# Pairs of score banks in one exp, the last denominators and two transposes in another order, and an ending on VectorE, in a four-layer cross-attention kernel

## The chip, the cores and the metric

The kernel runs on one core of one Trainium2 chip. The metric is device time in microseconds (us), the median of three runs. Engines are called by the names of the profile: PE is TensorE (PEld its weight loads), DVE is VectorE, ACT is ScalarE, POOL is GpSimd, SP issues the DMAs.

## What is computed

Eight sequences (a batch is one of them) pass through four layers of cross-attention with the same context:

```python
x = _L0(x, ctx)           # 16 heads of 64: softmax(q k / 8) v, Wo, + x, layer norm
x = _L1(ctx, x, mask)     # 16 heads of 16, keys = ctx and latents, out, rmsnorm, gelu MLP
x = _L2(x, ctx, mask)     # layer norm, 16 heads of 16, out, layer norm, gelu MLP
x = _L3(x, mask, ctx)     # 16 heads of 8, and with the mean also the spread of the values:
#   mean = softmax(..) v;  ex2 = softmax(..) v*v
#   std  = sqrt(relu(ex2 - mean*mean));  out = (instance_norm(x)*std + mean)*mask
```

Layers 0 and 3 have 256 columns of queries and 256 keys per head. They are the "first and last attention" whose exps the change touches.

## The kernel before

All five engines run their own instruction list, written out by hand, and wait for each other through semaphores. There is no scheduler: the order in the Python source of each engine is the order on the chip.

**Stages.** The list of one batch `b` is: projections of layer 1, its attention (`attention12`, L = 1), its MLP, the attention of layer 2, its MLP, and then the mixed stretch (`mixed`), in which layer 3 of batch `b` and layer 0 of batch `b + 1` alternate. Projections of the coming batch (`fill`) are put between the steps of the other stages as filling for PE.

**Scores and exps.** A step `k` of layer 0 or 3 makes the scores of a pair into the two PSUM banks `SC[0]` and `SC[1]` (`scores0`, `scores3`; L700 and L706, L794 and L798). ACT takes the exp of each bank, 512 columns, into one of the four slots of `Pr` (L1219 in layer 0, L1221 in layer 3, which has a bias column), and counts `p_ready` up after each. The next step's scores wait for `p_ready` of their own bank. The values are applied a step later (`pv0` L723, `pv3` L815). `pr_taken` keeps an exp from a slot of `Pr` that is still read.

**Row maxima.** Ahead of the scores, PE computes the same scores in bf16 for the maxima into two banks `MX` (L624, L639 and L645, L659 and L665), DVE reduces them (L1436), PE transposes the result (L678, L681, the units called "T"), and DVE copies the transposed maxima to `nmT` (L1423), which the scores of that group wait for.

**Denominators of layer 0.** Eight pairs of probability tiles are to be summed. POOL adds the two halves of a tile pair (`additions0`, L1769) into `Psum` for the first seven, PE sums over partitions from `Psum` (`denominators` L744), and the eighth pair comes straight from `Pr` (L741, twice as many matmuls). The table `BOTH` says in which step of the mixed stretch each of these stands: a row is (layer, step, units after the scores, units at the step's end). `("den", 3)`, the last denominators, stand at the end of step (3, 0). The table is read by PE, DVE and ACT alike.

**Layer 2's attention.** On PE the projection `k3` (L1091) stands between the scores of the first group and the transposed maxima of the second. On DVE, `quotient(b, 2, 0)` (L445, L1526, L1527: a reciprocal and a product) stands ahead of the copy of the maxima of layer 0's second group (L1423), for which `scores0(b + 1, 2)` waits (L700).

**The end of the program.** Layer 3's sums go to DRAM and back (`scratch`, `C3`), DVE takes a reciprocal (L1582), POOL makes the variance in five steps (L1709 to L1713), ACT loads the table of Sqrt and takes the root (L1261), then loads that of Exp again (L1262), and POOL makes the output in three steps (L1718 to L1720), which SP stores (L510). In the middle batches the same work lies beside the next batch's.

Of the kernel before, what the change touches and what calls it, by code (L numbers as in the profile page):

```python
# [29 lines left out]
B = 8  # L30
# [33 lines left out]
def alone(L):  # L64
# [8 lines left out]
        (3, 0, [], [("den", 3), (3, 1, 2)]),  # L73
        (3, 1, [(3, 1, "T"), ("recip", 1, 0)], [(0, 0, "B")]),
# [105 lines left out]
def build(nc, z_in, ctxT_in, ctx_in, mask1, mask2, mask3, w0, wo, w1qk, w1v, w1o, w1a, w1b,  # L180
          w2qkv, w2o, w2a, w2b, w3, cols_in, rows_in, ident_in, hmask_in, sel_in, out):
    with ExitStack() as stack:
# [127 lines left out]
        def row(name):  # L310
# [32 lines left out]
        v_step, p_step, f_step, x_step, v_apart, p_apart, n_apart, x_apart = (  # L343
            sem(n) for n in ("v_step", "p_step", "f_step", "x_step", "v_apart", "p_apart", "n_apart", "x_apart"))
# [106 lines left out]
        class Chain:  # L451
# [16 lines left out]
            def end(self):  # L468
                assert self.n == self.per_batch, self.n

# [98 lines left out]
        def _(pe):  # L569
# [159 lines left out]
            def denominators(b, m):  # L729
# [5 lines left out]
                pe.wait_ge(ps_ready, 7 * b + min(2 * m + 2, 7))  # L735
                n = SC_AT[b, 0, 14]
                for j in range(4):
                    dst = bank[32 * j:32 * j + 32, 0:D]
                    if m == 3 and j >= 2:
                        for kc in range(2):  # L740
                            mm = pe.matmul(dst, sums2[:, i, :], Pr[:, (n + j - 2) % 4, kc * D:kc * D + D],  # L741
                                           start=(i == 0), stop=True, skip_group_check=True)
                    else:
                        mm = pe.matmul(dst, sums2[:, i, :],  # L744
                                       Psum[:, (2 * m + j // 2) % 4, j % 2 * D:j % 2 * D + D],
                                       start=(i == 0), stop=True, skip_group_check=True)
# [202 lines left out]
            def body(b):  # L949
# [138 lines left out]
                def before2(i):  # L1088
                    if i == 0:
# [3 lines left out]
                def after2(i):  # L1093
                    if more:
# [3 lines left out]
                            lambda g, u: fill("vp3") if u == 0 and g == 0 else None, before2, after2)  # L1098
# [46 lines left out]
        def _(act):  # L1145
# [62 lines left out]
            def mixed(b, steps):  # L1208
                mix = mix_of(b)
                for i in steps:  # L1210
# [4 lines left out]
                    for j in range(2):  # L1215
# [41 lines left out]
            def std3(b):  # L1257
# [4 lines left out]
                act.activation(warm[:], half[:], ACT.Exp)  # L1262
# [127 lines left out]
            moments3(B - 1)  # L1390
            std3(B - 1)
# [3 lines left out]
        def _(dve):  # L1395
# [188 lines left out]
            def body(b):  # L1584
# [53 lines left out]
                quotient(b, 2, 0)  # L1638
                if more:
                    maxima(b + 1, 0, 1, "T")  # L1640
                quotient(b, 2, 1)
# [53 lines left out]
            end3(B - 1)  # L1695


        @block.gpsimd
        def _(pool):
# [5 lines left out]
            def end3(b):  # L1705

                ending.begin(b)
                pool.wait_ge(s_c3, b + 1)
                ending.step(pool.tensor_tensor(C3[:, 0, :], C3[:, 0, :], C3[:, 2, :], ALU.mult))  # L1709
                ending.step(pool.tensor_tensor(C3[:, 1, :], C3[:, 1, :], C3[:, 2, :], ALU.mult))  # L1710
                ending.step(pool.tensor_tensor(C3[:, 2, :], C3[:, 0, :], C3[:, 0, :], ALU.mult))
                ending.step(pool.tensor_tensor(C3[:, 1, :], C3[:, 1, :], C3[:, 2, :], ALU.subtract))
                pool.tensor_scalar(C3[:, 1, :], C3[:, 1, :], 0.0, None, ALU.max).then_inc(s_v, 1)  # L1713

            def output3(b):
                pool.wait_ge(s_std, b + 1)
                pool.wait_ge(s_xn, b + 1)
                ending.step(pool.tensor_tensor(C3[:, 3, :], C3[:, 3, :], xn[:], ALU.mult))  # L1718
                ending.step(pool.tensor_tensor(C3[:, 3, :], C3[:, 3, :], C3[:, 0, :], ALU.add))
                pool.tensor_tensor(C3[:, 3, :], C3[:, 3, :], m3[:], ALU.mult).then_inc(s_o3, 1)  # L1720
                ending.end()
# [51 lines left out]
            def body(b):  # L1773
# [37 lines left out]
                if not is_last(b):  # L1811
                    additions0(b + 1, [4, 5, 6])
# [108 lines left out]
```

## Time and profile before

| | us |
|---|---|
| median of 3 runs (1083.14 to 1083.92) | 1083.77 |
| the profiled execution | 1082.43 |
| its span, first to last instruction | 1080.6 |
| PE busy in it | 966.1 |
| DVE busy | 541.7 |
| ACT busy | 485.9 |
| POOL busy | 269.8 |
| one middle batch (start to start) | 126.0 |

The span is that of the profiled execution; what lies around it is 1.8 us. Busy times are sums of instruction durations. A matmul's duration runs past the start of the next, so the distance between the starts of two rows is what a group of matmuls costs PE, and that is how such rows are read below. "Idle" in brackets at the end of a row is how long the engine stood before it, and whose instruction released it.

### The profile page before, as it was taken

Reading aid. Unit: us, or ns where it says so; the run is one execution under the profiler, and the core shown is the slowest. Engines: PE = TensorE matmul, PEld = TensorE weight load, DVE = VectorE, ACT = ScalarE, POOL = GpSimd, SP = SyncE. Lnnn points to the kernel's source line nnn. Section 1 sums busy time; section 2 is a strip of 40 time slices with the busy share of each in tenths; the row PEclk is TensorE's granted clock in tenths of the full one; section 3 lists DMA queues with packets and bytes.
Section 4 is the critical chain, followed back from the end, with each engine's and each line's share of the span. In section 5 each row is a group of like instructions: output and inputs, shape, how many; then the busy total and the mean of one; then the engine's idle time right before and its main releaser. Section 6 shows DMA issues by size and latency. Waiting matters only on the chain.

```text
span 1080.6 us, 21561 instructions
## 1 busy us (share of the span) xinstructions
PE 966.1 (89%) x8592; PEld 603.1 (56%) x8592; DVE 541.7 (50%) x1028; ACT 485.9 (45%) x937; POOL 269.8 (25%) x389
## 2 busy tenths in 40 slices
PE   7989999999999999999999999999999999985671
PEld 5566663766455664666636665556646666344420
DVE  3343564455645565455644555455654556443440
ACT  2424453453534545445534545345454455433233
POOL 0220230242211611233202422116212332023203
PEclk9999999999999999999999999999999999988786
DMA  9300230011300212102300103002111022002000
GB/s 371 140 1 1 79 107 19 18 39 47 107 31 6 79 38 76 36 1 84 107 19 18 47 38 107 32 5 83 42 67 35 2 84 98 19 19 78 5 9 32
DMA packets 29058, 60.15 MB, mean 56 GB/s; under 512 B 9376, under 2 KB 21024, under 8 KB 24096
## 3 DMA queue, kind: packets, MB, share of 16 engines
q1 hardware_dynamic: 28960, 58.77, 15.1%
q8 instruction: 70, 1.15, 0.4%
q14 instruction: 28, 0.23, 0.1%
HBM read 53.52 MB, written 5.24 MB: 54 GB/s over the span
## 4 chain that ended last, share of the span: by engine, by line
PE 74%; DVE 10%; issue 10%; ACT 4%; POOL 2%; DMA 1%; POOLq 0%; SPq 0%; DVEq 0%; ACTq 0%
PE GP L584 6%; PE GP L992 6%; PE PV L723 6%; PE GP L1003 5%; PE GP L586 5%; PE SC L706 4%; DVE nm L1436 4%; PE SC L798 4%; PE GP L976 3%; PE PV L769 3%; PE GP L815 3%; PE SC L910 3%; PE GP L591 2%; PE PV L923 2%; PE GP L592 2%
## 5 line engine op out<-in xcount | busy, mean ns | idle before, releaser
L1436 DVE TENSOR_REDUCE nm<-MX 128x2 bf16<-128x512 f32 (+1 forms) x352 | 227.1, 689 | 152.2 <-PE MX L645 65.0
L1221 ACT ACTIVATE Pr<-SC,bcol 128x512 f32<-128x512 f32 x128 | 80.9, 683 | 132.9 <-PE SC L798 132.9
L584 PE MATMUL GP<-zP,W 128*128 128x128 f32 x512 | 106.9, 291 | 7.0 <-DMA W<-w 6.9
L1769 POOL TENSOR_TENSOR Psum<-Pr 128x512 f32<-128x512 f32 x56 | 71.3, 1273 | 163.6 <-ACT Pr L1219 163.6
L1219 ACT ACTIVATE Pr<-SC 128x512 f32<-128x512 f32 x128 | 69.2, 592 | 80.6 <-PE SC L706 80.6
L586 PE MATMUL GP<-uP,W 128*128 128x128 f32 x512 | 100.4, 278 | 0.0
L584 PEld LDWEIGHTS GP<-zP,W 128*128 128x128 f32 x512 | 78.9, 194 | 28.4 <-issue 26.7
L1253 ACT ACTIVATE Pr<-SC,bcol 128x512 f32<-128x512 f32 x96 | 60.7, 684 | 58.1 <-PE SC L910 58.1
L1737 POOL TENSOR_TENSOR stat<-stat,half 128x1 f32<-128x1 f32 x24 | 13.7, 569 | 269.8 <-DVE stat L1616 172.7
L586 PEld LDWEIGHTS GP<-uP,W 128*128 128x128 f32 x512 | 79.2, 195 | 0.0
L1003 PE MATMUL GP<-WB,work 128*128 128x256 f32 x256 | 60.8, 386 | 10.5 <-DVE work L1564 10.5
L723 PE MATMUL PV<-Pr,V 128*64 128x256 f32 x512 | 69.4, 392 | 0.8
L798 PE MATMUL SC<-work,K 64*128 64x512 f32 x256 | 67.7, 598 | 0.0
L1742 POOL TENSOR_TENSOR stat<-stat,half 128x2 f32<-128x2 f32 x8 | 5.7, 709 | 245.4 <-DVE stat L1492 245.4
L706 PE MATMUL SC<-Q,K 64*128 64x256 f32 x512 | 65.7, 376 | 0.0
L992 PE MATMUL GP<-oT,WA 128*128 128x128 f32 x512 | 64.0, 285 | 1.1 <-issue 0.8
L992 PEld LDWEIGHTS GP<-oT,WA 128*128 128x128 f32 x512 | 61.2, 199 | 5.0 <-issue 3.3
L1003 PEld LDWEIGHTS GP<-WB,work 128*128 128x128 f32 x256 | 46.8, 190 | 21.9 <-issue 16.5
L910 PE MATMUL SC<-work,K 64*128 64x512 f32 x192 | 54.3, 636 | 0.0
L1157 ACT ACTIVATE Q<-GP,cols 128x256 f32<-128x256 f32 x56 | 23.5, 470 | 68.4 <-PE GP L586 68.4
L1552 DVE TENSOR_TENSOR work<-GP,cols 128x512 f32<-128x512 f32 x32 | 22.1, 692 | 61.3 <-PE GP L992 61.3
L706 PEld LDWEIGHTS SC<-Q,K 64*128 64x128 f32 x512 | 49.3, 189 | 5.0
(194 smaller groups left out, 1727.4 us busy)
## 6 DMA issues: line engine op xcount, KB each, us to landing
WA<-w1a SPq DMA_DIRECT2D x8, 1024.0 KB, 4.8
WB<-w1b SPq DMA_DIRECT2D x8, 1024.0 KB, 7.0
WA<-w2a SPq DMA_DIRECT2D x8, 1024.0 KB, 5.0
WB<-w2b SPq DMA_DIRECT2D x8, 1024.0 KB, 7.1
W<-w SPq DMA_DIRECT2D x6, 1024.0 KB, 9.9
scratch<-U SPq DMA_DIRECT2D x16, 256.0 KB, 2.0
C<-scratch SPq DMA_DIRECT2D x96, 32.0 KB
zP<-z_in SPq DMA_DIRECT2D x8, 128.0 KB, 4.2
```

The lines of the kernel that those rows point to most:

```text
L584: pe.matmul(dst, W0[:, piece, 2 * s, at:at + P], zP[:, s * P:s * P + P], start=True, stop=False)
L586: mm = pe.matmul(dst, W0[:, piece, 2 * s + 1, at:at + P], uP[:, s * P:s * P + P], start=False, stop=True)
L706: mm = pe.matmul(SC[r][:, kc * D:kc * D + D], K0[half, k, kc * P:kc * P + P], Q0[half, k, :], start=False, stop=True, skip_group_check=True)
L723: mm = pe.matmul(bank[64 * j:64 * j + 64, i * D:i * D + D], V0[:, kc, h * 64:h * 64 + 64], Pr[:, (n + j) % 4, kc * D:kc * D + D], start=(k ...
L798: pe.matmul(SC[j][:].rearrange("p (t l) -> p t l", l=D), K3[half, g % 2, kc * P:kc * P + P], Q3[half, g // 2 * 2:g // 2 * 2 + 2, :], start ...
L910: pe.matmul(SC[r][:].rearrange("p (t l) -> p t l", l=P), K[half, c, kc * P:kc * P + P], Q12[half, 4 * c:4 * c + 4, :], start=False, stop=True,
L992: mm = pe.matmul(g[:, j * P:j * P + P], WA[:, c, f * P:f * P + P], oT[:, c, :], start=(c == 0), stop=(c == 1), skip_group_check=True)
L1003: mm = pe.matmul(g[:, 0:D], G[:, f * P:f * P + P], WB[:, f, :], start=(f == 0), stop=(f == 7))
L1219: act.activation(Pr[:, (n + j) % 4, :], SC[j], ACT.Exp, scale=0.125).then_inc(p_ready, 1)
L1221: act.activation(Pr[:, (n + j) % 4, :], SC[j], ACT.Exp, bias=bcol[:, 3 + k % 2:4 + k % 2], scale=8.0 ** -0.5).then_inc(p_ready, 1)
L1436: dve.tensor_reduce(dst, MX[(n + i) % 2][:].rearrange("p (a k) -> p a k", a=a), AX_X, ALU.max, negate=True).then_inc(mx_done, 1)
L1769: pool.tensor_tensor(Psum[:, c % 4, :].rearrange("p (a l) -> p a l", l=D), two[:, :, 0:D], two[:, :, D:2 * D], ALU.add)\
```

## The change

There are six edits.

1. In layers 0 and 3, ACT takes the exp of both score banks in one instruction of 1024 columns, once both banks are full, and counts `p_ready` up by two after it. There are 128 of these in place of 256 of 512 columns. Layers 1 and 2 keep theirs.
2. POOL adds the eighth pair too (64 additions L1769 in place of 56), and PE's last denominators come from `Psum` (four matmuls in place of six: the two L744 and four L741 become four of the first kind). The waits on `ps_ready` are renumbered, and ACT's wait on `den_done` goes.
3. `("den", 3)` moves from the end of step (3, 0) to the middle of step (3, 1), behind its scores.
4. `k3` moves from behind the scores of layer 2's first group to ahead of the maxima of its second group.
5. On DVE the copy of the maxima of layer 0's second group moves ahead of `quotient(b, 2, 0)`.
6. The last batch's eight steps on `C3` run on DVE in place of POOL. The Sqrt table is loaded by an extra small instruction right after `moments3`, and the last batch's return to the Exp table goes.

```diff
-        (3, 0, [], [("den", 3), (3, 1, 2)]),
-        (3, 1, [(3, 1, "T"), ("recip", 1, 0)], [(0, 0, "B")]),
+        (3, 0, [], [(3, 1, 2)]),
+        (3, 1, [("den", 3), (3, 1, "T"), ("recip", 1, 0)], [(0, 0, "B")]),
...
-                eng.wait_ge(ps_ready, 7 * b + min(u // 2 + 1, 7))
-                if u // 2 == 7:
-                    eng.wait_ge(den_done, 4 * b + 4)
+                eng.wait_ge(ps_ready, 8 * b + u // 2 + 1)
...
+        def variance3(eng, ending, b):
+            ending.begin(b)
+            ending.step(eng.tensor_tensor(C3[:, 0, :], C3[:, 0, :], C3[:, 2, :], ALU.mult))
...
+            eng.tensor_scalar(C3[:, 1, :], C3[:, 1, :], 0.0, None, ALU.max).then_inc(s_v, 1)
+        def scaled3(eng, ending):
+            ending.step(eng.tensor_tensor(C3[:, 3, :], C3[:, 3, :], xn[:], ALU.mult))
...
-                pe.wait_ge(ps_ready, 7 * b + min(2 * m + 2, 7))
-                n = SC_AT[b, 0, 14]
+                pe.wait_ge(ps_ready, 8 * b + 2 * m + 2)
                 for j in range(4):
                     dst = bank[32 * j:32 * j + 32, 0:D]
-                    if m == 3 and j >= 2:
-                        for kc in range(2):
-                            mm = pe.matmul(dst, sums2[:, i, :], Pr[:, (n + j - 2) % 4, kc * D:kc * D + D],
-                                           start=(i == 0), stop=True, skip_group_check=True)
...
-                def before2(i):
-                    if i == 0:
+                def amid2(g, u):
+                    if (g, u) == (0, 0):
+                        fill("vp3")
+                    if (g, u) == (0, "T"):
                         g, full = begin("k3", (ld_w3, 16))
...
+                    if L in (0, 3):
+                        act.wait_ge(sc_full, n + 2)
+                        pr_taken(act, n, 1)
+                        pr_taken(act, n + 1, 1)
+                        act.activation(Pr[:, n % 4:n % 4 + 2, :], SCP[:], ACT.Exp,
+                                       bias=bcol[:, 3 + k % 2:4 + k % 2] if L else 0.0,
+                                       scale=8.0 ** -0.5 if L else 0.125).then_inc(p_ready, 2)
...
-                act.activation(warm[:], half[:], ACT.Exp)
+                if not is_last(b):
+                    act.activation(warm[:], half[:], ACT.Exp)
...
             moments3(B - 1)
+            act.activation(warm[:], ident[:, 0:1], ACT.Sqrt)
             std3(B - 1)
...
+                if more:
+                    maxima(b + 1, 0, 1, "T")
                 quotient(b, 2, 0)
-                if more:
-                    maxima(b + 1, 0, 1, "T")
...
-                    additions0(b + 1, [4, 5, 6])
+                    additions0(b + 1, [4, 5, 6, 7])
...
             end3(B - 1)
+            last = Chain(dve, last_step, F_STEPS)
+            dve.wait_ge(s_c3, B)
+            variance3(dve, last, 0)
+            dve.wait_ge(s_std, B)
+            dve.wait_ge(s_xn, B)
+            scaled3(dve, last)
```

How the lists of the engines stand, before and now. First PE in the mixed stretch, from the values of step (0, 7) to the transposed maxima of step (3, 1); before:

```order
L723 MATMUL PV<-Pr,V 64x256 x3
L744 MATMUL PV<-Psum,sums 32x256 [waits ps_ready]
L744 MATMUL PV<-Psum,sums 32x256
L741 MATMUL PV<-Pr,sums 32x256 x4
L639 MATMUL MX<-b3row,sel 128x512 [waits mx_done]
L639 MATMUL MX<-b3row,sel 128x512
L645 MATMUL MX<-K3b,Q3b 128x256 x4
L794 MATMUL SC<-nmT,sel 128x256 [waits p_ready] x2
L794 MATMUL SC<-nmT,sel 128x256 x2
L798 MATMUL SC<-work,K 128x512 x2
L678 MATMUL MX<-identb,nm 128x128 [waits mx_done]
L678 MATMUL MX<-identb,nm 128x128
```

And in the changed kernel:

```order
L737 MATMUL PV<-Pr,V 64x256 [waits p_ready]
L737 MATMUL PV<-Pr,V 64x256 x3
L653 MATMUL MX<-b3row,sel 128x512 [waits mx_done]
L653 MATMUL MX<-b3row,sel 128x512
L659 MATMUL MX<-K3b,Q3b 128x256 x4
L801 MATMUL SC<-nmT,sel 128x256 [waits p_ready] x2
L801 MATMUL SC<-nmT,sel 128x256 x2
L805 MATMUL SC<-work,K 128x512 x2
L752 MATMUL PV<-Psum,sums 32x256 [waits ps_ready]
L752 MATMUL PV<-Psum,sums 32x256 x3
L692 MATMUL MX<-identb,nm 128x128 [waits mx_done]
L692 MATMUL MX<-identb,nm 128x128
```

The last denominators (32x256) stood ahead of the maxima and the scores of step (3, 1); they now stand behind them and ahead of the transposes, as four matmuls. `Psum` is POOL's sum, `sums` the ones that sum over partitions.

Next DVE behind layer 2's attention (`U<-PV` and `Ax` are the quotient, `nmT<-MX 128x256` is the copy of the maxima of layer 0); before:

```order
L1436 TENSOR_REDUCE nm<-MX 128x2 [waits mx_full0,mx_full1]
L1436 TENSOR_REDUCE nm<-MX 128x2
L445 TENSOR_TENSOR gate<-half 128x1 [waits v_apart,pv_done,s_Ax]
L1526 RECIPROCAL U<-PV 128x128
L1527 TENSOR_TENSOR Ax<-PV,U 128x128 [waits v_step]
L1423 COPY nmT<-MX 128x256 [waits mx_full1]
L445 TENSOR_TENSOR gate<-half 128x1 [waits v_apart,pv_done,s_Ax]
L1526 RECIPROCAL U<-PV 128x128
L1527 TENSOR_TENSOR Ax<-PV,U 128x128 [waits v_step]
```

And in the changed kernel:

```order
L1455 TENSOR_REDUCE nm<-MX 128x2 [waits mx_full0,mx_full1]
L1455 TENSOR_REDUCE nm<-MX 128x2
L1442 COPY nmT<-MX 128x256 [waits mx_full1]
L443 TENSOR_TENSOR gate<-half 128x1 [waits v_apart,pv_done,s_Ax]
L1545 RECIPROCAL U<-PV 128x128
L1546 TENSOR_TENSOR Ax<-PV,U 128x128 [waits v_step]
L443 TENSOR_TENSOR gate<-half 128x1 [waits v_apart,pv_done,s_Ax]
L1545 RECIPROCAL U<-PV 128x128
L1546 TENSOR_TENSOR Ax<-PV,U 128x128 [waits v_step]
```

The copy moved up over one quotient's three instructions.

Last ACT at the end of the program (`C<-C` is the root, `warm` a column that only calls for a table); before:

```order
L1182 ACTIVATE Ax,stat<-m 128x256 [waits s_nst]
L1261 ACT_TABLE_LOAD [waits st_out,s_v]
L1261 ACTIVATE C<-C 128x256 [waits s_nst]
L1262 ACT_TABLE_LOAD
L1262 ACTIVATE warm<-half 128x1
```

And in the changed kernel:

```order
L1192 ACTIVATE Ax,stat<-m 128x256 [waits s_nst]
L1409 ACT_TABLE_LOAD
L1409 ACTIVATE warm<-ident 128x1 [waits s_nst]
L1278 ACTIVATE C<-C 128x256 [waits st_out,s_v]
```

The table load that stood between the wait for `s_v` and the root now stands ahead of that wait.

## Rows read from the trace of the kernel before

**Rows 1.** Windows, two batches: us, busy PE, PEld, DVE, ACT, POOL; clock, DMA

```profile
198.00:324.00 126.00, 119.10 (x1077) 74.30 (x1076) 67.41 (x129) 60.89 (x118) 33.85 (x48) 1.00 0.14 49
...
954.00:1081.00 127.00, 74.29 (x644) 43.85 (x642) 46.71 (x89) 41.36 (x78) 28.56 (x49) 0.81 0.08 27
```

**Rows 2.** Page, the chain that ended last, shares by engine

```profile
PE 74%; DVE 10%; issue 10%; ACT 4%; POOL 2%; DMA 1%; POOLq 0%; SPq 0%; DVEq 0%; ACTq 0%
```

**Rows 3.** Timeline, TensorE, batch 3: start, us, line, what, count [idle <-releaser]

```profile
537.82 0.64 PE L744 MATMUL PV<-Psum,sums 128*32 128x256 f32 x8
538.39 0.29 PE L678 MATMUL MX<-identb,nm 128*128 128x128 bf16 x2
...
540.07 0.38 PE L794 MATMUL SC<-nmT,sel 64*128 64x256 bf16 x4
...
541.24 1.08 PE L723 MATMUL PV<-Pr,V 128*64 128x256 f32 x8
542.25 0.41 PE L744 MATMUL PV<-Psum,sums 128*32 128x256 f32 x2
...
543.26 0.39 PE L639 MATMUL MX<-b3row,sel 64*128 64x512 bf16 x2
...
543.71 0.38 PE L794 MATMUL SC<-nmT,sel 64*128 64x256 bf16 x4
...
545.45 0.27 PE L678 MATMUL MX<-identb,nm 128*128 128x128 bf16 x2 [0.50 <-DVE nm L1436]
```

**Rows 4.** Timeline, same place: GpSimd, ScalarE, VectorE

```profile
536.45 1.27 POOL L1769 TENSOR_TENSOR Psum<-Pr 128x512 f32<-128x512 f32 x1 [1.37 <-ACT Pr L1219]
...
541.35 1.26 ACT L1221 ACTIVATE Pr<-SC,bcol 128x512 f32<-128x512 f32 x2 [1.43 <-PE SC L798]
...
544.01 1.29 DVE L1436 TENSOR_REDUCE nm<-MX 128x2 bf16<-128x512 f32 x2 [2.35 <-PE MX L645]
```

**Rows 5.** Timeline, TensorE, the end of the third attention

```profile
503.56 0.70 PE L1091 MATMUL GP<-uC,W 128*128 128x256 f32 x2
504.09 0.22 PE L681 MATMUL MX<-identb,nm 128*128 128x128 bf16 x1
...
507.22 0.29 PE L678 MATMUL MX<-identb,nm 128*128 128x128 bf16 x2
...
509.02 0.39 PE L700 MATMUL SC<-nmT,sel 64*128 64x512 bf16 x2 [0.50 <-DVE nmT L1423]
...
510.20 1.13 PE L984 MATMUL GP<-W2O,Ax 128*128 128x256 f32 x4
511.44 1.08 PE L723 MATMUL PV<-Pr,V 128*64 128x256 f32 x8
...
515.44 0.71 PE L1110 MATMUL GP<-W,uC 128*128 128x128 f32 x4 [0.32 <-ACT Q L1157]
```

**Rows 6.** Timeline, VectorE, the same stretch

```profile
508.68 0.28 DVE L1423 COPY nmT<-MX 128x256 bf16<-128x256 bf16 x1
...
509.93 0.29 DVE L1527 TENSOR_TENSOR Ax<-PV,U 128x128 f32<-128x128 f32 x1
```

**Rows 7.** Timeline, all engines, the end of the program

```profile
1070.33 0.72 POOL L1709 TENSOR_TENSOR C<-C 128x256 f32<-128x256 f32 x1 [3.47 <-DVE C L1582]
...
1074.37 1.28 ACT L1261 ACT_TABLE_LOAD   x1 [12.21 <-issue]
...
1076.16 0.72 POOL L1718 TENSOR_TENSOR C<-C,xm 128x256 f32<-128x256 f32 x1 [1.86 <-ACT C L1261]
...
1078.51 0.34 SPq L510 DMA_DIRECT2D out<-C  x1
```

**Rows 8.** Groups by line and shape: busy us, mean ns, idle before

```profile
L1219 ACT ACTIVATE Pr<-SC 128x512 f32<-128x512 f32 x128 | 69.2, 592 | 80.6 <-PE SC L706 80.6
...
L1613 DVE TENSOR_TENSOR xa<-GP,res 128x256 f32<-128x256 f32 x8 | 3.4, 425 | 8.8 <-PE GP L984 8.8
...
L1621 DVE TENSOR_SCALAR xb<-xa,stat 128x256 f32<-128x256 f32 x8 | 2.8, 353 | 4.1 <-POOL stat L1737 4.1
```

More of the change, by code:

```diff
@@ L469, in end @@
                 assert self.n == self.per_batch, self.n
+        def variance3(eng, ending, b):
+            ending.begin(b)
+            ending.step(eng.tensor_tensor(C3[:, 0, :], C3[:, 0, :], C3[:, 2, :], ALU.mult))
+            ending.step(eng.tensor_tensor(C3[:, 1, :], C3[:, 1, :], C3[:, 2, :], ALU.mult))
+            ending.step(eng.tensor_tensor(C3[:, 2, :], C3[:, 0, :], C3[:, 0, :], ALU.mult))
+            ending.step(eng.tensor_tensor(C3[:, 1, :], C3[:, 1, :], C3[:, 2, :], ALU.subtract))
+            eng.tensor_scalar(C3[:, 1, :], C3[:, 1, :], 0.0, None, ALU.max).then_inc(s_v, 1)
+        def scaled3(eng, ending):
+            ending.step(eng.tensor_tensor(C3[:, 3, :], C3[:, 3, :], xn[:], ALU.mult))
+            ending.step(eng.tensor_tensor(C3[:, 3, :], C3[:, 3, :], C3[:, 0, :], ALU.add))
+            eng.tensor_tensor(C3[:, 3, :], C3[:, 3, :], m3[:], ALU.mult).then_inc(s_o3, 1)
+            ending.end()
         def shifts(b, L, g):
@@ L734, in denominators @@
                     wait(pe, *pv_bank_taken(b, "den", half))
-                pe.wait_ge(ps_ready, 7 * b + min(2 * m + 2, 7))
-                n = SC_AT[b, 0, 14]
+                pe.wait_ge(ps_ready, 8 * b + 2 * m + 2)
                 for j in range(4):
                     dst = bank[32 * j:32 * j + 32, 0:D]
-                    if m == 3 and j >= 2:
-                        for kc in range(2):
-                            mm = pe.matmul(dst, sums2[:, i, :], Pr[:, (n + j - 2) % 4, kc * D:kc * D + D],
-                                           start=(i == 0), stop=True, skip_group_check=True)
[L743 to L746, printed above, removed]
+                    mm = pe.matmul(dst, sums2[:, i, :], Psum[:, (2 * m + j // 2) % 4, j % 2 * D:j % 2 * D + D],
+                                   start=(i == 0), stop=True, skip_group_check=True)
                 mm.then_inc(den_done, 1)
@@ L1097, in body @@
                 attention12(b, 2, make, K2, lambda g, t, kc: V2[:, slot(g, t):slot(g, t) + 32], (s_V2, b + 1),
-                            lambda g, u: fill("vp3") if u == 0 and g == 0 else None, before2, after2)
+                            amid2, after=after2)
                 if more:
@@ L1214, in mixed @@
                         queries3(b, [(Q3, 0), (Q3, 1)])
-                    for j in range(2):
+                    if L in (0, 3):
[5 more added lines that the diff above has]
+                                       scale=8.0 ** -0.5 if L else 0.125).then_inc(p_ready, 2)
+                    for j in range(0 if L in (0, 3) else 2):
                         act.wait_ge(sc_full, n + j + 1)
@@ L1637, in body @@
                     maxima(b + 1, 0, 1, 2)
-                quotient(b, 2, 0)
                 if more:
                     maxima(b + 1, 0, 1, "T")
+                quotient(b, 2, 0)
                 quotient(b, 2, 1)
@@ L1705, in end3 @@
             def end3(b):
-                ending.begin(b)
                 pool.wait_ge(s_c3, b + 1)
[L1709 to L1713, printed above, removed]
+                variance3(pool, ending, b)
             def output3(b):
@@ L1717, in output3 @@
                 pool.wait_ge(s_xn, b + 1)
[L1718 to L1721, printed above, removed]
+                scaled3(pool, ending)
             def blocks12(b, L):
@@ L1825, in _ @@
             pool.wait_ge(const_p, 3)
-            additions0(0, range(7))
+            additions0(0, range(8))
             power0(0)
```

6 lines of the change are left out of this document (2 added, 4 removed).

## The prediction

> **What bounds the kernel now.** I read four views, in this order: windows by batch, the chain that ended last, the timeline around each moved instruction, and the timeline of the program's end. In a middle batch PE is busy 119.1 of 126.0 us at full clock, and no other engine passes 67.4; in the last batch PE is busy 74.3 of 127 us and the granted clock averages 0.81 [rows 1]. The chain that ended last is PE for 74% [rows 2]. So seven of eight batches are PE's list plus the few places in which PE stands, and the last batch and the end of the program are latencies, one engine after another. ACT is busy 60.9 of 126 us: shortening it pays only where PE waits for an exp. What counts is what leaves PE's list, which of PE's gaps is filled, and what leaves the chain at the end.
>
> **Edits 2 and 3: the last denominators.** They cost PE from 542.25 to 543.26, 1.01 us; the denominators that come from `Psum` alone cost from 537.82 to 538.39, 0.57 [rows 3]. So the form saves 0.44. The move saves more. Today the transposes at 545.45 wait 0.50 for DVE's reductions, which start 0.75 behind the maxima (543.26 to 544.01) and let PE go 1.44 after their start [rows 3, 4]. In the new order, from 542.25: maxima 0.45 (543.26 to 543.71), scores 1.17 (as 540.07 to 541.24), denominators 0.57, together 2.19 [rows 3]; DVE's side is 0.75 + 1.44 = 2.19 as well. The transposes start at 544.44 in place of 545.45: 1.0 us less, because the denominators now lie in the gap. Behind them the list is the same and relative to itself, so the gain stays. Seven mixed stretches have these denominators: 7.0 us. Bounds: 0 (something else catches up at once) and 1.0 each; I take 1.0, since both sides of the row agree. The first batch's prologue has no such gap and saves the form alone, 0.4.
>
> What the edit can spoil: POOL's eighth addition must be done before them. An addition takes 1.27 and starts about as the exp ends [rows 4]; the scores of step (0, 7) are in by 537.82, where the next work starts [rows 3], their exp by 539.0, so `Psum` is ready near 540.3, 3.5 us ahead of its new reader. In the prologue the reader is not moved, and there one addition can be late, 1.27 at most and once. ACT no longer waits for `den_done`, which the move would otherwise have made late.
>
> **Edit 5: the copy ahead of the quotient.** The transposed maxima are made at 507.22, but DVE copies them at 508.68 behind a quotient, and the scores stand 0.50 for it until 509.02 [rows 5, 6]. With the copy first (near 507.5) the scores start at 508.5 when PE is free. The second quotient, which ends at 510.22 today (509.93 + 0.29, rows 6), ends 0.1 later, since it gains the copy's place and loses the copy's wait; the second half of the output projection can go at about 510.5, as today within 0.2 us. The next thing PE waited for is the exp of these scores: the values at 511.44 come 1.24 behind the projection at 510.20 [rows 5], and they follow the exp, so they come 0.45 earlier. The `v3` matmuls at 515.44 waited 0.32 for ACT's `Q` [rows 5], which follows the filling behind these values, so they follow too. Gain 0.45, bounds 0.15 (layer norm after the second quotient holds the rest) and 0.5; seven times, 3.2 us.
>
> **Edit 4: `k3`.** It costs PE 503.56 to 504.09, 0.53 [rows 5]. It leaves a place between scores and transposes that wait for DVE's two reductions (1.3 us, as in rows 4), and goes to one where PE stands for DVE's copy of the transposed maxima. It fills one gap and opens another, both set by DVE: I take 0.04 each, 0.3 in all, nearest to nothing; bounds 0 and 0.53 each, its whole cost hidden.
>
> **Edit 1: one exp over two banks.** One exp of 512 columns is 592 ns [rows 8], the pair with a bias 1.26 us [rows 4]. The trace has no exp of 1024 columns: it costs at least one (0.68) and at most two separately (1.37 with the bias); I take 1.12, the pair without one start, nearest to the 1.26. The Trainium skill, "ScalarE: Activation LUTs", section "What ACT_TABLE_LOAD costs", gives 280 ns and 0.833 ns a column with a pointer bias, an estimate of 1.13 us; by it the sum below is the same. The one exp starts when the second bank is full, about 0.1 later, and ends about when the second does today. The first bank comes free 0.4 later, and that is the price where PE has nothing else. Tightest is step (3, 1): exp from 541.45 to 542.57 against scores at 542.70. The slack is 0.1. In the other steps maxima and values (over 1 us) lie between. In the last four steps of the last batch the chain runs through both exps and scores, and shortens by some 0.05 each. Denominators (0, 5) behind a slightly later evacuation may lose 0.05 a batch. Net I take a loss of 0.2, bounds +2 and -2.
>
> **Edit 6: the end.** From 1070.33 to 1074.37 are POOL's five steps, 4.04 us; then the table 1.28; the root to 1076.16; then three steps, 2.35, to 1078.51 [rows 7]. Nearest DVE rows at 256 columns: 425 ns for two tensors, 353 ns with a scalar [rows 8]; with 0.04 for a wait on itself, five steps are 4 x 0.46 + 0.35 = 2.2, three are 1.35. The table load goes under ACT's idle stretch of 12.21 [rows 7]. Gain 1.85 + 1.28 + 1.0 = 4.1, bounds 3.3 (DVE's steps at 0.6 each) and 4.5. The load row, 1.28, stands with ACT idle before and the root right behind. The Trainium skill, same page and section, puts about 1.38 us of drain to each switch, which would make 5.5; the distance from 1074.37 to 1076.16 has no room for it.
>
> **The sum.** 7.0 + 0.4 + 3.2 + 0.3 - 0.2 + 4.1 = 14.8. The profiled execution took 1082.43 us, so 1067.6; it was 1.3 below the median, so **1069 us**.
>
> The last batch starts 11 us earlier, and there PE works at half clock (1.2 of 2.4 GHz) in parts: a mean of 0.81 over 127 us is up to 48 us at half, so 24 lost at most, of which 14 by PE's busy share of 74.3 in 127 [rows 1]. Which matmuls fall there may change; a fifth of it is 3 us either way. The Trainium skill, "TensorE: Matmul & The Clock Gate", part 1, says that PE's activity releases the throttle; the trace agrees (1.00 where PE is busy 119 of 126, rows 1), and it changes no term here.
>
> **Rivals.**
> - *The gains on PE are taken back by the next wait.* For it: DVE and ACT sit close behind PE in the mixed stretch, both sides of my 2.19 are equal, and one tenth of slack stands at (3, 1). Against: behind each place PE runs on without idle in the rows. Then remain the form, 0.44 x 8 = 3.5, the quotient at its lower bound 1.1, the end 4.1: 8.7, so 1075.
> - *Only the end pays.* If every gap re-forms (POOL's longer list holds the denominators, edit 5 delays layer norm), 4.1: 1079.6.
> - *The exp over both banks holds PE, slower.* PE starts the next scores on the first bank while ACT is on the second; now they wait for both. If PE has nothing between, each step costs 0.44 (the later release of bank 0). It decides from 14.8 / 0.44 = 34 of the 128 steps. If half of them, 64, are such steps: 28 us, 1097. For it: the closed ring at the end of the last batch. Against: PE's place after the scores has maxima or values in every middle step.
> - *The switch costs its drain too* and the end gives 5.5: 1067.5.
>
> **How the numbers follow.** Forecast 0.63, gains taken back 0.22, only the end 0.05, exp slower 0.05, drain 0.05. The range reaches from 1065 (drain or a kind clock) to 1076.5 (gains taken back, with an unkind clock). A difference under 0.2%, 2.2 us, could not be told from none by this measurement. Faster by more: 0.93; slower by more: 0.05 (the exp ring); between: 0.02.
>
> **What would show it.** In the new profile: transposes of step (3, 1) about 2.2 us behind the values of step (0, 7) and no idle before them; the period of a middle batch 124.5 in place of 126.0; no wait of layer 0's third scores for the copy; exps of 1024 columns at 1.03 and 1.12; 8.2 us from the reciprocal's end to the store becoming 4.1. I am wrong if the period stays above 125.3, if PE shows new idle before scores released by ACT, or if the exp takes 1.3 and more.

## The result and the profile after

The changed kernel takes 1071.75 us (median of 4 runs, 1070.70 to 1075.57) against 1083.85 (4 runs, 1083.14 to 1085.31): a ratio of 0.9887, 95% interval 0.9867 to 0.9907. The forecast was 1069, range 1065 to 1076.5. So it is faster, by 12.1 us where 14.8 were forecast. The profiled execution took 1071.56 (span 1069.8). Of the runs below, one of the twelve of the copy-first kernel took 1442.0 us at a mean granted clock of 0.62, and it is left out of that kernel's figures.

The windows of a middle and of the last batch, which answer to [rows 1] (the middle one is now 124.4 us wide), and the chain's shares, as [rows 2]:

```profile
196.40:320.80 124.40, 118.49 (x1071) 73.67 (x1071) 67.22 (x128) 59.23 (x102) 35.51 (x50) 1.00 0.14 50
943.20:1069.80 126.60, 77.90 (x647) 45.39 (x645) 49.93 (x97) 38.94 (x69) 24.13 (x42) 0.80 0.08 28
```

```profile
PE 74%; DVE 11%; issue 7%; ACT 4%; POOL 2%; DMA 1%; SPq 0%; DVEq 0%; ACTq 0%; POOLq 0%
```

Where the 10.87 us between the two profiled executions lie I read from the starts of `q1`, the first matmuls of each batch (L976 before, L983 after). Two of them in the profile after, TensorE's timeline:

```profile
442.88 1.38 PE L983 MATMUL GP<-hT,W1QK 128*128 128x128 f32 x9
```

```profile
567.52 1.81 PE L983 MATMUL GP<-hT,W1QK 128*128 128x128 f32 x11
```

| stretch, us | before | after | change | forecast |
|---|---|---|---|---|
| start to the first `q1` | 69.89 | 69.83 | -0.06 | -0.4 |
| a typical middle batch | 125.77 | 124.37 | -1.40 | -1.5 |
| seven batches, first to last `q1` | 879.63 | 869.78 | -9.85 | -10.1 |
| last batch, `q1` to PE's last matmul | 110.46 | 114.07 | +3.61 | -0.2, clock 3 either way |
| PE's last matmul to the end | 20.63 | 16.10 | -4.53 | -4.1 |

(The batch shown is 124.64 long, the longest of the seven; the same one before is 126.05. The 126.0 of the prediction was the width of a window. The forecast's loss of 0.2 for the exp is spread here as its text has it: 0.05 lost in each of eight batches at the denominators (0, 5), 0.05 gained in each of the last four steps.) The middle batches and the end did what was forecast. The miss is nearly all in one row: the last batch, up to PE's last matmul, took 3.6 us longer in these two executions.

**The denominators**, TensorE and ScalarE, the place of [rows 3, 4]:

```profile
536.56 1.08 PE L737 MATMUL PV<-Pr,V 128*64 128x256 f32 x8
537.57 0.39 PE L653 MATMUL MX<-b3row,sel 64*128 64x512 bf16 x2
...
539.19 0.64 PE L752 MATMUL PV<-Psum,sums 128*32 128x256 f32 x8
539.76 0.28 PE L692 MATMUL MX<-identb,nm 128*128 128x128 bf16 x2
```

```profile
536.75 1.11 ACT L1229 ACTIVATE Pr<-SC,bcol 128x1024 f32<-128x1024 f32 x1 [1.52 <-PE SC L805]
```

The values of step (0, 7) start at 536.56, the transposes of (3, 1) at 539.76, 3.20 later; before it was 4.21 (541.24 to 545.45, rows 3). From the end of the values (537.57) it is 2.19, the 2.2 of the forecast. The denominators cost 539.19 to 539.76, 0.57, and the transposes have no idle time in brackets any more. This is the 1.0 of the forecast.

**The copy ahead of the quotient**, VectorE and TensorE, the place of [rows 5, 6]:

```profile
503.23 0.29 DVE L1442 COPY nmT<-MX 128x256 bf16<-128x256 bf16 x1 [1.05 <-PE MX L692]
...
504.49 0.29 DVE L1546 TENSOR_TENSOR Ax<-PV,U 128x128 f32<-128x128 f32 x1
```

```profile
504.14 0.39 PE L714 MATMUL SC<-nmT,sel 64*128 64x512 bf16 x2
```

The copy starts at 503.23, now ahead of the quotient's last step (504.49), and the third scores start at 504.14 without waiting.

**The exps**, groups by form, as [rows 8] (busy us, mean ns):

```profile
L1229 ACT ACTIVATE Pr<-SC,bcol 128x1024 f32<-128x1024 f32 x64 | 71.2, 1113 | 137.0 <-PE SC L805 126.1 <-issue 10.9
L1229 ACT ACTIVATE Pr<-SC 128x1024 f32<-128x1024 f32 x64 | 65.3, 1020 | 81.9 <-PE SC L720 42.4 <-issue 39.5
```

1020 and 1113 ns, where the prediction says 1.03 and 1.12. The Trainium skill, "ScalarE: Activation LUTs", section "What ACT_TABLE_LOAD costs", gives an estimate of 1.04 without the pointer bias and 1.13 with it, both 0.02 too long here.

**The end**, ScalarE, VectorE and SyncE, the place of [rows 7]:

```profile
1055.85 1.28 ACT L1409 ACT_TABLE_LOAD   x1
1057.15 0.20 ACT L1409 ACTIVATE warm<-ident 128x1 f32<-128x1 f32 x1
...
1063.67 0.42 DVE L472 TENSOR_TENSOR C<-C 128x256 f32<-128x256 f32 x1
...
1065.51 0.29 DVE L476 TENSOR_SCALAR C<-C 128x256 f32<-128x256 f32 x1
1065.84 0.42 ACT L1278 ACTIVATE C<-C 128x256 f32<-128x256 f32 x1 [8.49 <-DVE C L476]
...
1067.66 0.34 SPq L524 DMA_DIRECT2D out<-C  x1
```

From the first step behind the reciprocal (1063.67) to the store it is 3.99 us; it was 8.18 before (1070.33 to 1078.51, rows 7). VectorE's five steps take 2.17 to the root's start, as forecast 2.2. The table is loaded at 1055.85, 10 us ahead of the root. The other 0.3 of the 4.53 in the table lies ahead of the reciprocal, which starts 8.19 us behind PE's last matmul in place of 8.51.

### The profile page after: what moved, and what is told of

The parts are those of the page before. It is cut to its first block, busy times and chain, and to the rows that moved or that the text cites. A ratio compares the mean times of both kernels' runs of the same rounds, so it can differ in the third digit from the quotient of the medians.

```text
span 1069.8 us, 21418 instructions
## 1 busy us (share of the span) xinstructions
PE 965.6 (90%) x8560; PEld 600.5 (56%) x8560; DVE 545.0 (51%) x1036; ACT 471.2 (44%) x808; POOL 275.1 (26%) x389
## 4 chain that ended last, share of the span: by engine, by line
PE 74%; DVE 11%; issue 7%; ACT 4%; POOL 2%; DMA 1%; SPq 0%; DVEq 0%; ACTq 0%; POOLq 0%
PE GP L598 6%; PE GP L999 6%; PE PV L737 6%; PE GP L1010 6%; PE GP L600 5%; PE SC L805 5%; DVE nm L1455 4%; PE SC L720 4%; PE GP L983 3%; PE PV L776 3%; PE PV L930 3%; PE GP L822 2%; PE GP L605 2%; PE SC L917 2%; PE MX L653 2%
## 5 line engine op out<-in xcount | busy, mean ns | idle before, releaser
L1229 ACT ACTIVATE Pr<-SC,bcol 128x1024 f32<-128x1024 f32 x64 | 71.2, 1113 | 137.0 <-PE SC L805 126.1
L1786 POOL TENSOR_TENSOR Psum<-Pr 128x512 f32<-128x512 f32 x64 | 81.4, 1272 | 173.6 <-ACT Pr L1229 173.6
L1229 ACT ACTIVATE Pr<-SC 128x1024 f32<-128x1024 f32 x64 | 65.3, 1020 | 81.9 <-PE SC L720 42.4
L1270 ACT ACTIVATE Pr<-SC,bcol 128x512 f32<-128x512 f32 x96 | 60.7, 684 | 58.6 <-PE SC L917 58.6
L1754 POOL TENSOR_TENSOR stat<-stat,half 128x1 f32<-128x1 f32 x24 | 13.7, 569 | 267.7 <-DVE stat L1635 172.5
L1442 DVE COPY nmT<-MX 128x256 bf16<-128x256 bf16 (+1 forms) x96 | 25.8, 269 | 55.1 <-PE MX L692 40.2
L1571 DVE TENSOR_TENSOR work<-GP,cols 128x512 f32<-128x512 f32 x32 | 22.1, 692 | 59.5 <-PE GP L999 59.5
```

The costliest lines, as they stand in the source:

```text
L1229: act.activation(Pr[:, n % 4:n % 4 + 2, :], SCP[:], ACT.Exp, bias=bcol[:, 3 + k % 2:4 + k % 2] if L else 0.0, scale=8.0 ** -0.5 if L else ...
L1270: act.activation(Pr[:, n % 4, :], SC[n % 2][:], ACT.Exp, bias=bias, scale=scale)\
L1786: pool.tensor_tensor(Psum[:, c % 4, :].rearrange("p (a l) -> p a l", l=D), two[:, :, 0:D], two[:, :, D:2 * D], ALU.add)\
```

## The experiments

Each kernel was timed together with the kernel before, and its ratio is to that kernel's times there. "Period" is the length of a typical middle batch. "Half clock" is the time at 1.2 GHz in the last batch's first 100 us or to PE's last matmul, from the granted clock: in a window of 25 us with a mean of 0.86 it is 50 x (1 - 0.86) = 7 us, since the clock granted is either 1.2 or 2.4 GHz.

**One edit at a time, from the kernel before.**

The last denominators, in the new form and at the new place, edits 2 and 3:

```diff
-        (3, 0, [], [("den", 3), (3, 1, 2)]),
-        (3, 1, [(3, 1, "T"), ("recip", 1, 0)], [(0, 0, "B")]),
+        (3, 0, [], [(3, 1, 2)]),
+        (3, 1, [("den", 3), (3, 1, "T"), ("recip", 1, 0)], [(0, 0, "B")]),
...
-            additions0(0, range(7))
+            additions0(0, range(8))
```

> The kernel before with the last denominators alone (edits 2 and 3: from Psum in one pass, and one step later). By the theory that they then lie in the gap before the transposes of step (3, 1): period of a middle batch 125.77 - 1.0 = 124.8, seven times, and 0.2 in the prologue (there the projection of the attention then waits for ScalarE's evacuation): 7.2 us less, about 1076.5. By the rival that the next wait takes the move back: only the form, 0.44 a batch, period 125.3, about 1080.5.

Measured: 1077.67, ratio 0.9932 (0.9919 to 0.9946); period 124.79; seven batches 872.71, 6.92 less. The rival is out.

The form alone, which is edit 2 with the table as before (the expectation calls it edit 3):

```diff
-                    if m == 3 and j >= 2:
...
-            additions0(0, range(7))
+            additions0(0, range(8))
```

> The kernel before with the form alone (edit 3: eight additions and one kind of denominators, at their old place). By my theory PE's list is shorter by 0.44 a batch and the transposes of (3, 1) still wait 0.50 for DVE, whose reductions start with the maxima behind the denominators: period 125.35, 3.3 us in all, about 1080.5. By the rival that POOL's eighth addition (1.27) comes too late for a reader at the old place, about 0.9 behind the values of (0, 7): PE waits up to 0.5 there and the gain is nothing, period 125.8 or more, about 1084.

Measured: 1079.98, ratio 0.9960 (0.9944 to 0.9975); period 125.33, so the form alone is 0.44 and the move 0.54. TensorE's timeline shows both halves:

```profile
541.00 0.64 PE L736 MATMUL PV<-Psum,sums 128*32 128x256 f32 x8
541.57 0.39 PE L637 MATMUL MX<-b3row,sel 64*128 64x512 bf16 x2
...
543.75 0.27 PE L676 MATMUL MX<-identb,nm 128*128 128x128 bf16 x2 [0.50 <-DVE nm L1427]
```

The denominators cost 0.57 at their old place, with no wait for POOL, and the transposes still stand 0.50. The rival, POOL too late, is out.

The copy first, edit 5:

```diff
+                if more:
+                    maxima(b + 1, 0, 1, "T")
                 quotient(b, 2, 0)
-                if more:
-                    maxima(b + 1, 0, 1, "T")
```

> The kernel before with edit 5 alone (the copy of the transposed maxima ahead of the first quotient). By the forecast 0.45 a batch: period 125.3, 3.2 us in all, about 1080.7. By the rival that the second quotient and layer norm take it back: 0.15 a batch, about 1082.8.

Measured: 1083.32 against 1085.12, ratio 0.9983 (0.9969 to 0.9997); period 125.36, 0.41 a batch, 2.93 in the seven. The medians' interval, 0.3 to 3.4 us, has room for both the forecast and the rival; the period, 0.41 against the rival's 0.15, decides for the forecast.

One exp over both banks, edit 1:

```diff
+                    if L in (0, 3):
+                        act.wait_ge(sc_full, n + 2)
...
+                    for j in range(0 if L in (0, 3) else 2):
```

> The kernel before with edit 1 alone (one exp over both banks in the first and the last attention). By the forecast nothing in the middle batches (period 125.8, within 0.1) and within 0.3 in all, about 1084; the last four steps of the last batch stay at 2.50 to 2.55. By the rival that the missing 3 us of the last batch are the exp's, which frees the first bank later: the last batch is 2 to 3 us longer from its first matmul to the end, 1086 to 1087.

Measured: 1085.41 against 1085.12, ratio 1.0006 (0.9993 to 1.0019); period 125.77 and seven batches 879.63, to the hundredth as before. Its cost is in the last steps of the last batch, TensorE's timeline:

```profile
1059.36 0.39 PE L794 MATMUL SC<-nmT,sel 64*128 64x256 bf16 x4 [0.71 <-ACT Pr L1219]
...
1061.90 0.64 PE L815 MATMUL GP<-Pr,V 128*32 128x256 f32 x8 [0.72 <-ACT Pr L1219]
```

The last scores wait 0.71 for the exp, and the last values 2.54 behind them wait for it again; the last six steps are mostly 2.50 apart with two exps of 512 and 2.55 to 2.63 with one (K part to K part). From the first scores of this attention (1038.34) to the first matmul of the last values (1061.90) it is 23.56 against 23.39 with the clock alike: 0.17 lost. In this profile the whole last batch is 112.9 us, 2.5 more than before, which is the rival's number; but the rest of it came with 41.0 us at half clock against 34.1, and the medians of 11 and 23 runs are alike. So the exp costs 0.2 here, and not the missing 3 us.

The end, edit 6:

```diff
             moments3(B - 1)
+            act.activation(warm[:], ident[:, 0:1], ACT.Sqrt)
...
+            variance3(dve, last, 0)
...
-            end3(B - 1)
-            output3(B - 1)
```

> The kernel before with edit 6 alone (the last steps on VectorE, the Sqrt table loaded early). Nothing else moves, so the whole 4.1 us come out at the end: 8.2 from the reciprocal to the store becomes 4.1, about 1079.7. By the rival that the changed end itself costs the last batch its missing 3 us: about 1082.7.

Measured: 1080.83 against 1084.55, ratio 0.9962 (0.9948 to 0.9976), 4.1 us. PE's last matmul to the end: 16.21, 4.4 less. The rival is out.

This run is also a control. Its instructions up to PE's last matmul are those of the kernel before, and still its profiled execution has 113.7 us from the last `q1` to there, 3.3 more than the 110.5 before, with 44.4 us at half clock against 34.1. Two executions of one and the same last batch can differ by nearly as much as the +3.61 of the table.

`k3` moved, edit 4:

```diff
-                def before2(i):
-                    if i == 0:
+                def amid2(g, u):
+                    if (g, u) == (0, 0):
+                        fill("vp3")
+                    if (g, u) == (0, "T"):
                         g, full = begin("k3", (ld_w3, 16))
```

> The kernel before with edit 4 alone (k3 behind the first transposes of the third attention). Middle batches: 0.00 to 0.04 less each. Last batch: k3 stands in front of the second pair of maxima; at half clock that pair starts 0.5 to 0.6 later behind the transposes than in the kernel before, and the second scores some 0.3 later; at full clock under 0.1. In all 0 to 0.5 slower, about 1085.

Measured: 1086.63 against 1083.95, ratio 1.0028 (1.0011 to 1.0046): slower by about 3 us, more than any theory had. In the middle batches nothing (period 125.81, against 125.77; 0.11 us in seven). So all of it is in the last batch. It is not only a lower mean clock: at a mean of 0.973 two executions of this kernel took 1086.49 and 1086.63, and the four of the kernel before timed beside them 1083.60 to 1084.50.

The changed kernel with `k3` back (the reverse of that diff):

> The changed kernel with k3 back at its old place (edit 4 undone). In the middle batches within 0.05 a batch either way (forecast 0.04 gained by the edit), so the period is 124.4 to 124.5. In the last batch k3 is 0.65 us of half-clock work in front of the second pair of maxima: by the theory that the move costs there, the last batch is 0.4 to 0.7 shorter, about 1071.3. By the theory that the clock alone makes the last batch's loss, its length depends on where the half-clock stretches fall, 1070 to 1073 with no direction.

Measured: 1071.21, ratio 0.9875 (0.9859 to 0.9891), period 124.37. The intervals with and without the move overlap, so this run decides for neither theory, and the 3 us of the move alone are not seen between these two medians (1071.75 and 1071.21). The direct cost can be read. TensorE, third attention of the last batch, the changed kernel and then this one:

```profile
990.94 0.27 PE L695 MATMUL MX<-identb,nm 128*128 128x128 bf16 x1 [1.57 <-DVE nm L1455]
991.07 1.19 PE L1101 MATMUL GP<-uC,W 128*128 128x256 f32 x2
992.19 0.61 PE L673 MATMUL MX<-b2row,sel 64*128 64x512 bf16 x2
...
996.28 0.21 PE L913 MATMUL SC<-nmT,sel 64*128 64x128 bf16 x1 [0.70 <-ACT Pr L1270]
996.77 0.39 PE L913 MATMUL SC<-nmT,sel 64*128 64x128 bf16 x7 [0.28 <-ACT Pr L1270]
```

```profile
991.35 0.27 PE L695 MATMUL MX<-identb,nm 128*128 128x128 bf16 x1 [1.57 <-DVE nm L1452]
992.03 0.61 PE L673 MATMUL MX<-b2row,sel 64*128 64x512 bf16 x2 [0.41 <-DVE nmT L1439]
...
995.23 1.22 PE L1098 MATMUL GP<-uC,W 128*128 128x256 f32 x2
...
996.88 0.45 PE L913 MATMUL SC<-nmT,sel 64*128 64x128 bf16 x8 [0.32 <-DVE nmT L1439]
```

Both stretches start at half clock. At its new place `k3` takes 1.12 (991.07 to 992.19) in a gap of 0.41, so the second maxima come 1.25 behind the transposes in place of 0.68. At its old place it lay under the wait for the exp, which now stands open (0.70). The second scores (all but their first matmul) are 5.83 behind the transposes against 5.53: 0.3 lost. The rest of the 3 us of `k3` alone I can't place by a row. More half-clock time followed in the profile of that kernel (58 us against 34), but it is of the slowest of its eight executions (1091.74), which doesn't prove that the move caused it.

**The clock in the last batch.** PE stands there for VectorE and ScalarE in every step. These kernels put matmuls of the identity, whose results nothing reads, into those waits, in the last batch alone. They go to a bank of PSUM that the next real matmuls overwrite:

```diff
+PADS = {"oT": 14, "w2": 8, "yT": 20, "q2": 6, "yT2": 20, "w4": 20, "q3": 4}
...
                     pe.wait_ge(*o.bank_taken(name))
+                    for _ in range(PADS.get(name, 0) if is_last(b) else 0):
+                        pe.matmul(GP[bank][:, 0:P], ident[:], ident[:], start=True, stop=True)
                     for s, v in ready:
```

> The kernel before with 92 matmuls more in the last batch, 128x128 of the identity, put where PE waits for VectorE or ScalarE (14 ahead of oT, 8 of w2, 20 each of yT, yT2 and w4, 6 of q2, 4 of q3), into a bank that the next matmuls overwrite. They compute nothing. If the clock is what the waiting costs, the 41.4 us at half clock in the last batch shrink to under 15 and the last batch gets 3 to 10 us shorter. If the clock doesn't follow PE's activity there, the pads only lengthen the waits: 0 to 4 us longer.

> The changed kernel with the same 92 matmuls in its last batch. By the theory that the missing 3 us of its last batch are half-clock time, both padded kernels have about the same clock there, and the difference between them is the forecast's sum of 13 to 15 us. By the rival that the edits themselves (k3, the exp) cost the last batch 3 us, the difference stays at 12 (1071.75 against 1083.85).

Measured: 1084.55 against 1084.55 (ratio 0.9996, 0.9984 to 1.0008) and 1071.69 (0.9877, 0.9861 to 0.9893), a difference of 12.9. Half clock fell (23.9 and 20.5 us, from 34.1 and 41.0; the 41.4 of the expectation isn't what the profile of the kernel before shows up to PE's last matmul) and the time did not, so neither expectation was met: I had sized a pad at 0.11 us. TensorE's timeline of the changed kernel without pads, then with 92, then with 47:

```profile
983.64 0.41 PE L975 MATMUL GP<-ident,xb 128*128 128x128 f32 x2 [3.04 <-DVE xb L1593]
```

```profile
980.72 4.63 PE L970 MATMUL GP<-ident 128*128 128x128 f32 x40
985.18 0.38 PE L978 MATMUL GP<-ident,xb 128*128 128x128 f32 x2
```

```profile
979.22 2.62 PE L970 MATMUL GP<-ident 128*128 128x128 f32 x22
982.34 0.44 PE L978 MATMUL GP<-ident,xb 128*128 128x128 f32 x2 [0.50 <-DVE xb L1596]
```

Twenty pads take 4.46 (980.72 to 985.18), 0.22 each (the trace has two records for each); the wait was 3.04. So they made the batch wait for them. Eleven end 0.50 before VectorE does. The difference of 12.9 can't be held against 14 or 12: its interval is wider than both.

The run with 47, the changed kernel and `PADS = {"oT": 8, "w2": 4, "yT": 11, "q2": 3, "yT2": 11, "w4": 10}`:

> The changed kernel with 47 matmuls of the identity in the last batch instead of 92 (8 ahead of oT, 4 of w2, 11 of yT, 3 of q2, 11 of yT2, 10 of w4), each 0.23 us, so that at full clock they end within the waits they lie in (2.37, 1.38, 3.04, 0.99, 3.04, 2.87). The theory that the waiting costs clock: half-clock time in the last batch falls to 20 to 25 us as with 92, but now without the 1.0 to 1.5 that the long rows of pads cost, so 2 to 4 us less than the changed kernel, about 1069. The rival, that the clock gained is worth nothing since the batch waits for VectorE and ScalarE: 1071 to 1072.

Measured: 1065.73 (1064.26 to 1067.30), ratio 0.9834 (0.9820 to 0.9848), 6 us less than the changed kernel, with 17.1 us at half clock against 41.0. The rival is out, and the gain is more than the 2 to 4 of the theory.

The next fills the waits for the maxima too, with 31 more, and takes `k3` back:

```diff
+            def idle_work(b, name, count):
+                if is_last(b):
+                    bank, _ = order_of(b).at(name)
+                    pe.wait_ge(*order_of(b).bank_taken(name))
+                    for _ in range(count):
+                        pe.matmul(GP[bank][:, 0:P], ident[:], ident[:], start=True, stop=True)
...
                         for name in entry(b):
+                            idle_work(b, "u0", 3 if name[2] == 0 else 5)
                             unit(*name)
...
+                        if (i, name) == (0, (3, 1, 2)):
+                            idle_work(b, "u0", 5)
                         unit(*name)
```

> As the run before, with k3 back at its old place and 29 to 31 more such matmuls in the waits for the maxima (5 in the second attention, 8 in the third, 11 and 5 in the last one's start). If those waits are what lowers the clock there, the two steps of the last attention that ran at half clock run at full, scores' spacing 4.0 and 2.6 in place of 5.6 and 3.5; with that 4 to 6 us less than the changed kernel, 1066 to 1068.

Measured: 1059.01 (1058.50 to 1060.62), ratio 0.9771 (0.9759 to 0.9784): 25 us under the kernel before, and beyond the expectation. The windows of the last batch's first 100 us, the changed kernel, then this one (columns as in [rows 1]):

```profile
939.60:964.60 25.00, 21.23 (x232) 12.93 (x232) 12.44 (x23) 7.01 (x13) 6.38 (x10) 0.86 0.03 10
964.60:989.60 25.00, 14.98 (x84) 12.27 (x82) 9.13 (x20) 8.24 (x17) 10.42 (x19) 0.84 0.23 85
989.60:1014.60 25.00, 15.60 (x144) 10.59 (x144) 11.24 (x24) 6.72 (x13) 5.87 (x9) 0.82 0.02 6
1014.60:1039.60 25.00, 18.09 (x96) 8.79 (x97) 9.18 (x16) 6.52 (x12) 0.72 (x1) 0.66 0.00 1
```

```profile
940.20:965.20 25.00, 22.12 (x250) 14.72 (x251) 12.86 (x24) 7.20 (x14) 6.50 (x10) 0.93 0.04 11
965.20:990.20 25.00, 21.36 (x167) 17.95 (x166) 11.62 (x23) 8.12 (x17) 14.13 (x23) 1.00 0.22 85
990.20:1015.20 25.00, 20.82 (x196) 16.69 (x194) 11.17 (x24) 8.11 (x16) 3.58 (x6) 1.00 0.02 6
1015.20:1040.20 25.00, 21.60 (x194) 10.22 (x192) 11.52 (x20) 10.57 (x14) 0.00 (x0) 1.00 0.05 17
```

PE is busy 20.8 to 22.1 of 25 us in place of 15.0 to 21.2, and the granted clock is 1.00 in three of the four in place of 0.84, 0.82 and 0.66. Half clock: 7 + 8 + 9 + 17 = 41 us against 3.5. The first scores of the last attention show what that is worth, the changed kernel and then this one:

```profile
1027.58 0.37 PE L692 MATMUL MX<-identb,nm 128*128 128x128 bf16 x2 [1.55 <-DVE nm L1455]
1028.34 0.61 PE L801 MATMUL SC<-nmT,sel 64*128 64x256 bf16 x4 [0.39 <-DVE nmT L1442]
1028.74 1.92 PE L805 MATMUL SC<-work,K 64*128 64x512 f32 x4
1030.44 0.64 PE L653 MATMUL MX<-b3row,sel 64*128 64x512 bf16 x2
```

```profile
1017.34 1.38 PE L962 MATMUL GP<-ident 128*128 128x128 f32 x10
1018.97 0.27 PE L693 MATMUL MX<-identb,nm 128*128 128x128 bf16 x2 [0.25 <-DVE nm L1472]
...
1019.86 1.02 PE L806 MATMUL SC<-work,K 64*128 64x512 f32 x4
1020.72 0.38 PE L654 MATMUL MX<-b3row,sel 64*128 64x512 bf16 x2
```

From the first `K` part to the second and on to the third it is 3.68 and 2.96 here, against 5.57 and 3.52 in the changed kernel (expected: 4.0 and 2.6). The scores' `K` part takes 1.70 (1028.74 to 1030.44) at half clock and 0.86 (1019.86 to 1020.72) at full. The pads of 1017.34 end before VectorE's reduction lets the transposes go, 0.25 to spare.

And with two exps again (edit 1 undone):

> As the run before, with edit 1 undone as well (two exps of 512 columns). The ring of the last eight steps loses the 0.18 that the one exp costs there (23.81 against 23.63 from the first scores to the last values, at one clock); the middle batches stay at 124.3 to 124.4. About 0.2 less than the run before. By the rival that the one exp pays in the middle, the batches are longer than 124.4.

Measured: 1059.82, ratio 0.9779 (0.9767 to 0.9792), the same as the run before within the measurement. In the traces the last attention, from its first scores to its last values, is 21.91 against 22.08, 0.17 less as expected, and the seven batches are 869.78 against 869.77: the one exp neither costs nor pays in the middle.

The last batch of these profiles, from `q1` to PE's last matmul:

| kernel | half clock | length, us |
|---|---|---|
| before | 34.1 | 110.5 |
| denominators, form and place | 37.5 | 111.3 |
| denominators, form alone | 30.7 | 110.2 |
| copy first | 30.7 | 110.3 |
| one exp alone | 41.0 | 112.9 |
| the end alone | 44.4 | 113.7 |
| `k3` alone | 58.0 | 119.9 |
| changed | 41.0 | 114.1 |
| changed, `k3` back | 37.5 | 111.3 |
| before, 92 pads | 23.9 | 113.5 |
| changed, 92 pads | 20.5 | 113.0 |
| changed, 47 pads | 17.1 | 106.4 |
| more pads, `k3` back | 3.4 | 102.2 |
| the same, two exps | 3.4 | 102.0 |

## Why the prediction came out as it did

**What bounds the kernel: right.** PE's list in seven batches, latencies in the last one and at the end. The gains came from the places named: 9.85 us in the seven batches, 4.5 at the end.

**Edits 2 and 3: right.** 6.92 against 7.0, and the equal sides of the gap held: POOL's addition was in time. In the prologue the forecast 0.4 became 0.2. TensorE after the change:

```profile
57.12 0.64 PE L752 MATMUL PV<-Psum,sums 128*32 128x256 f32 x8
57.92 1.13 PE L776 MATMUL PV<-A0a,WO 128*128 128x256 f32 x4 [0.15 <-ACT work L1197]
```

The form went from 1.00 to 0.64, but the projection then waits 0.15 for ScalarE: 0.80 in all. And PE's first matmul, which waits for the DMA of the weights, started 0.21 later in this execution (7.15 against 6.94), which leaves the -0.06 of the table.

**Edit 5: right in mechanism, 0.41 against 0.45 a batch**, 2.9 us against 3.2.

**Edit 6: right**, 4.1 in its own run and 4.2 from reciprocal to store. Rival four is out. The load takes 1.28, and the next instruction starts 0.02 behind it (1055.85 to 1057.15). The 1.38 us of drain at each switch, which the prediction quotes from the Trainium skill, "ScalarE: Activation LUTs", section "What ACT_TABLE_LOAD costs", isn't seen there.

**Edit 1: sign and size right by luck.** The 0.2 was priced as a late evacuation in all batches (0.4), less 0.2 gained in the last ring. The evacuation cost nothing: the seven batches are 879.63 in both kernels. The last ring lost 0.2 instead, since the scores of the next step wait for the whole exp. The rival needed 34 slower steps; only those of the last ring show it, at -0.02 to +0.12 each.

**Edit 4: wrong.** The step that failed is "it fills one gap and opens another, both set by DVE: I take 0.04 each". I worked it out from a middle batch at full clock, where it came to 0.00, and applied it to the last batch unseen, where `k3` takes 1.12 and the gap is 0.41. Alone it costs 3.0 us (1.2 to 5.0, from the ratio), of which a row shows 0.3; within the changed kernel its cost is 0.5 between medians, less than the noise.

**The clock: named, not priced.** "Which matmuls fall there may change; a fifth of it is 3 us either way." The changed profile had 41.0 us at half clock against 34.1, and it fell on dense work. The `WB` matmuls, the changed kernel and the one with `k3` back:

```profile
1014.69 5.38 PE L1010 MATMUL GP<-WB,work 128*128 128x256 f32 x16 [2.87 <-DVE work L1583]
```

```profile
1015.64 3.69 PE L1010 MATMUL GP<-WB,work 128*128 128x256 f32 x16 [2.87 <-DVE work L1580]
```

5.38 against 3.69: 1.69 of the 2.8 us between these two last batches is this one row, and the kernel before had it at full clock too. The first two steps of the last attention, 5.57 and 3.52 from `K` part to `K` part against 5.00 and 2.96 before, are another 1.1 with more time at half clock (the scores' `K` part alone is 1.70 or 0.86). With 0.2 for the exp and 0.3 for `k3` itself that is 3.3 of the +3.61. That half-clock time is worth this much is shown by the pads: 47 matmuls whose results nothing reads take 6 us from the changed kernel, and 78 take 12.2 from the one with `k3` back (1071.21 to 1059.01).

Whether the edits caused the clock's shift isn't shown. The kernel with the new end alone, whose last batch no edit touches up to PE's last matmul, has +3.3 in its profile, so the whole +3.61 may be the execution's own. The profile of the kernel before, from which the forecast was made, is on the kind side: 54 runs of that kernel, timed beside the twelve, have a median of 1084.5 and spread from 1081.6 to 1088.2. Between medians, 12.1 us (10.1 to 14.4) stand against 14.8. Of that miss of 2.7 the rows name 0.2 in the prologue, 0.3 in the seven batches and 0.3 for `k3` in the last, against which the end gave 0.4 more; for the rest no run shows a cause.

## What to carry to other kernels

Price an edit separately in each stage in which its instruction runs: a move that is free where the engine is full can cost where it waits for others, and there the clock multiplies it. Where PE waits often, what it does while waiting sets how fast it works next; matmuls for nothing, 78 of them sized under the measured waits (here 0.22 us each, against waits of 1.0 to 3.0), gave 12.2 us, as much as all six edits together. Before a miss is put down to an edit, compare a stretch that the edit doesn't touch: here it moved by 3.3 us by itself. Judge edits of under 3 us by the period in the trace, not by a median.

## What the hardware showed that I had not expected

- No wait of PE in the changed kernel's last batch, up to its last matmul, is longer than 3.04 us, and still 41 of 114 us were at 1.2 GHz. In the stretch from 1014.60 PE was busy 18.09 of 25 us with a granted clock of 0.66; in the same stretch of the kernel with more pads it was busy 21.60 and the clock 1.00. The Trainium skill, "TensorE: Matmul & The Clock Gate", part 1, says that PE's activity releases the throttle. These runs agree, and where the prediction says that it changes no term, it was worth more than any term.
- The mean granted clock tells executions of one kernel apart. Of the 54 runs of the kernel before timed beside the experiments, the ten at 0.978 average 1082.6 us and the nine at 0.971 average 1086.0.
- Half-clock time has no fixed price. Between the copy-first kernel and the one with the new end it is 3.5 us of length for 13.7 at half clock, 0.25 each. In the `WB` row, dense matmuls at a mean granted clock of 0.68 (3.4 us of 5.38 at half), it is 1.69, 0.5 each.
- An exp of 1024 columns over two PSUM banks is 1113 ns with a pointer bias and 1020 without; two of 512 are 1.26 us and 1.08. ScalarE saved 0.15 and 0.06 a pair and the kernel nothing.
